# Rows of four tokens per partition, statistics by bn_aggr and a shorter warm-up in a gated mixer with routed experts

## What is computed

```python
xn = layernorm(x)                                   # per token over 128 channels
# mixer: six projections of x + (prev - x) * mix, a scan over time, a group norm of 8 channels
state = state * decay + alpha * k * v ; mixed = r * state
s = (groupnorm(mixed) * gn_w + gn_b) * g @ W_out.T + b_out
# experts: four rounds; 4 experts of 128 -> 512 -> 128, the best two of each token mixed by softmax
for r in range(4):
    logits = cur @ Wg[r] + bg[r]
    cur = cur + sum_e cw[:, e] * (gelu(cur @ W1[e] + b1[e]) @ W2[e] + b2[e])
out = x + s * silu(cur)
```

## Time and profile before

| what | value |
|---|---|
| median of 3 runs | 806.81 us (806.5 to 807.61) |
| the profiled execution's own time | 807.0 us |
| its span, first to last instruction | 804.9 us |
| PE busy | 793.4 us, 99% of the span |
| DVE busy | 711.7 us, 88% |
| ACT busy | 651.9 us, 81% |
| DMA, HBM traffic | 40.34 MB read, 2.36 MB written |

### The profile page before, as it was taken

How to read it: one execution, slowest core, us unless ns; L and a number is a source line. 1 busy time by engine, 2 the same in 40 slices (tenths; PEclk the granted TensorE clock), 3 DMA queues, 4 the chain that set the end, 5 groups by cost and what they waited for, 6 DMA issues and landing times.

```text
span 804.9 us, 10652 instructions
## 1 busy us (share of the span) xinstructions
PE 793.4 (99%) x3668; PEld 638.2 (79%) x3668; DVE 711.7 (88%) x1328; ACT 651.9 (81%) x912; POOL 114.8 (14%) x135
## 2 busy tenths in 40 slices
PE   7999999999999999999999999999999999999997
PEld 6778788887888878888788887888788887778785
DVE  6989888889998989889998889998989898998888
ACT  6899888877888877888788887888778877878775
POOL 0021111111111111111111111121111111111110
PEclk9999999999999999999999999999999999999999
DMA  9444362432532416333164422644236443174532
GB/s 258 121 89 133 67 188 49 106 92 40 146 83 61 101 31 155 96 57 89 33 152 98 101 40 42 142 105 100 46 62 155 100 118 66 28 184 118 132 66 52
DMA packets 44468, 78.50 MB, mean 98 GB/s; under 512 B 6656, under 2 KB 23552, under 8 KB 40448
## 3 DMA queue, kind: packets, MB, share of 16 engines
q0 software_dynamic: 18144, 33.04, 24.3%
q1 hardware_dynamic: 25136, 44.64, 17.1%
q10 hardware_dynamic: 1136, 0.16, 0.1%
HBM read 40.34 MB, written 2.36 MB: 53 GB/s over the span
## 4 chain that ended last, share of the span: by engine, by line
PE 88%; DVE 5%; ACT 2%; DMA 2%; issue 1%; SPq 0%; DVEq 0%; ACTq 0%
PE h_bank L910 13%; PE h_bank L906 13%; PE h_bank L907 13%; PE y_bank L971 13%; PE y_bank L967 13%; PE y_bank L966 13%; DVE g_lo L639 2%; PE p_bank L906 2%; PE p_bank L910 2%; PE p_bank L907 2%; PE r_bank L1005 1%; ACT g L401 1%; DMA cw_b<-in_w 1%; PE p_bank L936 1%; ACT g_hi L405 1%
## 5 line engine op out<-in xcount | busy, mean ns | idle before, releaser
L401 ACT ACTIVATE g<-h_bank,b_c 128x512 f32<-128x512 f32 x512 | 329.6, 682 | 71.8 <-PE h_bank L910 70.3
L639 DVE TENSOR_TENSOR g_lo<-g,g_hi 128x1024 fp32r<-128x1024 f32 x256 | 308.6, 1221 | 63.4 <-ACT g_hi L405 62.5
L405 ACT ACTIVATE g_hi<-g 128x1024 fp32r<-128x1024 f32 x256 | 271.9, 1062 | 8.1
L341 POOL DMA_DIRECT2D cur<-tmp x126 | 113.6, 902 | 677.7 <-DVE tmp L653 553.0
L906 PE MATMUL h_bank<-cur_hi,w_hi 128*128 128x512 f32 x512 | 205.9, 402 | 1.2 <-ACT g L401 0.7
L910 PE MATMUL h_bank<-cur_lo,w_hi 128*128 128x512 f32 x512 | 203.6, 398 | 0.0
L907 PE MATMUL h_bank<-cur_hi,w_lo 128*128 128x512 f32 x512 | 202.3, 395 | 0.0
L967 PE MATMUL y_bank<-g_hi,w_lo 128*128 128x512 f32 x508 | 200.6, 395 | 0.0
L966 PE MATMUL y_bank<-g_hi,w_hi 128*128 128x512 f32 x508 | 200.5, 395 | 0.0
L971 PE MATMUL y_bank<-g_lo,w_hi 128*128 128x512 f32 x508 | 139.3, 396 | 0.0
L910 PEld LDWEIGHTS h_bank<-cur_lo,w_hi 128*128 128x128 f32 x512 | 96.2, 188 | 23.5 <-DVE cur_lo L588 0.4
(11 more groups left out here) (133 smaller groups left out, 497.4 us busy)
## 6 DMA issues: line engine op xcount, KB each, us to landing
cur<-tmp POOLq DMA_DIRECT2D x126, 256.0 KB, 3.4
cw_b<-cw_scratch SPq DMA_DIRECT2D x31, 1024.0 KB, 5.1
cur<-in_x SPq DMA_DIRECT2D x8, 256.0 KB, 5.6
xn_t<-cur SPq DMA_DIRECT2D x8, 256.0 KB, 2.9
xr<-in_x SPq DMA_DIRECT2D x8, 256.0 KB, 3.2
out<-o SPq DMA_DIRECT2D x7, 256.0 KB, 2.4
cw_b<-in_w SPq DMA_DIRECT2D x4, 256.0 KB, 6.1
cw_b<-cw_scratch SPq DMA_DIRECT2D x1, 768.0 KB, 5.3
```

The costliest lines, as they stand in the source:

```text
L341: pool.dma_start(cur[:, block_of(s // E)], tmp[:, s % SUMS, :], accum_op=ALU.add).then_inc(summed, DMA)
L401: nc.scalar.activation(g[:, gb, ft * BLK:(ft + 1) * BLK], hb[ft][:, :], ACT.Gelu_apprx_tanh, bias=b1_c[:, e * FT + ft:e * FT + ft + 1]).th ...
L405: nc.scalar.activation(g_hi[:, gb, h], g[:, gb, h], ACT.Copy).then_inc(g_hi_done, 1)
L639: nc.vector.tensor_tensor(g_lo[:, gb, h], g[:, gb, h], as_f32(g_hi[:, gb, h]), ALU.subtract).then_inc(g_lo_done, 1)
```

## The change

The rows of x and of the output that a DMA moves become four tokens of one partition: partition p holds tokens 4p to 4p + 3 of its block, one row of 2048 bytes in memory (block 7: two tokens, 1024 bytes, for each half). A tile t then holds every fourth token, so `turn_normed` writes column t, t + 4, ... of its bank, and `turn_product` reads such columns of `th`; the rest of the kernel sees tokens in their old order. For blocks 0 and 1 mean and variance come from bn_aggr, block by block. The warm-up is 26 transposes and then 15, one behind each of DVE's first 15 linked steps.

```diff
-WARM_UP, FILL = 52, 4
+WARM_UP, FILL = 26, 4
+ROOT_CHAIN = 15
...
+        mv = sb("mv", [128, 2 * TPB, 2])
...
+        def by_partition(b, rows):
+            if b < NB - 1:
+                return rows.rearrange("(p t) d -> p t d", t=TPB)
+            return rows.rearrange("(n p t) d -> p n t d", n=2, t=TPB // 2)
+        def tokens_of(b, t):
+            if b < NB - 1:
+                return slice(t, BLK, TPB)
+            n, i = t // (TPB // 2), t % (TPB // 2)
+            return slice(n * HALF + i, (n + 1) * HALF, TPB // 2)
...
-                             x[c * BLK:(c + 1) * BLK, :].rearrange("(t p) d -> p t d", p=128)).then_inc(x_loaded[c], DMA)
+                             by_partition(c, x[c * BLK:(c + 1) * BLK, :])).then_inc(x_loaded[c], DMA)
...
-            sp.dma_start(out[(NB - 1) * BLK:(NB - 1) * BLK + BLK // 2, :].rearrange("(t p) d -> p t d", p=128),
+            sp.dma_start(out[(NB - 1) * BLK:(NB - 1) * BLK + BLK // 2, :].rearrange("(p t) d -> p t d", t=TPB // 2),
...
+            def norm_first():
+                for b in (0, 1):
+                    norm_stats((b,))
+                    for c in range(b * TPB, (b + 1) * TPB):
+                        last = nc.vector.bn_aggr(mv[:, c, :], stats[:, c, :])
+                    link(last)
+                h = tiles_of((0, 1))
+                link(nc.vector.tensor_scalar(veps[:, h], mv[:, :, 1], LN_EPS, None, ALU.add))
+                nc.vector.tensor_scalar(mean[:, h], mv[:, :, 0], 1.0, None, ALU.mult)
...
-            norm_stats((0, 1))
-            norm_spread((0, 1))
+            norm_first()
...
-                    ins = nc.tensor.transpose(pb[:, t * D:(t + 1) * D], xn_st[:, b % 2, t * D:(t + 1) * D], ident[:, :])
+                    ins = nc.tensor.transpose(pb[:, tokens_of(b, t)], xn_st[:, b % 2, t * D:(t + 1) * D], ident[:, :])
...
-                    ins = nc.tensor.transpose(rb[:, t * D:(t + 1) * D], th[:, b % 2, t * D:(t + 1) * D], ident[:, :])
+                    ins = nc.tensor.transpose(rb[:, t * D:(t + 1) * D], th[:, b % 2, tokens_of(b, t)], ident[:, :])
...
             for _ in range(WARM_UP):
                 nc.tensor.transpose(rb[:, 0:D], ident[:, :], ident[:, :])
+            for n in range(ROOT_CHAIN):
+                pe.wait_ge(dve_step, n + 1)
+                nc.tensor.transpose(rb[:, 0:D], ident[:, :], ident[:, :])
             turn_normed(0)
```

More of the change, by code:

```diff
@@ L226, in block_of, with by_tile @@
             return slice(k % NB * BLK, (k % NB + 1) * BLK)
+        def by_partition(b, rows):
+            if b < NB - 1:
+                return rows.rearrange("(p t) d -> p t d", t=TPB)
+            return rows.rearrange("(n p t) d -> p n t d", n=2, t=TPB // 2)
+        def by_tile(b, ap):
+            if b < NB - 1:
+                return ap.rearrange("p (t d) -> p t d", t=TPB)
+            return ap.rearrange("p (n t d) -> p n t d", n=2, t=TPB // 2)
+        def tokens_of(b, t):
+            if b < NB - 1:
+                return slice(t, BLK, TPB)
+            n, i = t // (TPB // 2), t % (TPB // 2)
+            return slice(n * HALF + i, (n + 1) * HALF, TPB // 2)
         block = ctx.enter_context(nc.Block())
@@ L232, in load_x @@
             def load_x(c):
-                sp.dma_start(cur[:, block_of(c)].rearrange("p (t d) -> p t d", t=TPB),
-                             x[c * BLK:(c + 1) * BLK, :].rearrange("(t p) d -> p t d", p=128)).then_inc(x_loaded[c], DMA)
+                sp.dma_start(by_tile(c, cur[:, block_of(c)]),
+                             by_partition(c, x[c * BLK:(c + 1) * BLK, :])).then_inc(x_loaded[c], DMA)
             def load_w1(e):
@@ L286, in load_x_again @@
                     sp.wait_ge(r_empty, r_jobs["end", b - 2] + 1)
-                sp.dma_start(xr[:, b % 2, :].rearrange("p (t d) -> p t d", t=TPB),
-                             x[b * BLK:(b + 1) * BLK, :].rearrange("(t p) d -> p t d", p=128)).then_inc(x_again[b % 2], DMA)
+                sp.dma_start(by_tile(b, xr[:, b % 2, :]),
+                             by_partition(b, x[b * BLK:(b + 1) * BLK, :])).then_inc(x_again[b % 2], DMA)
             def store(b):
                 sp.wait_ge(r_empty, r_jobs["end", b] + 1)
-                sp.dma_start(out[b * BLK:(b + 1) * BLK, :].rearrange("(t p) d -> p t d", p=128),
-                             o[:, b % 2, :].rearrange("p (t d) -> p t d", t=TPB)).then_inc(stored[b % 2], DMA)
+                sp.dma_start(by_partition(b, out[b * BLK:(b + 1) * BLK, :]),
+                             by_tile(b, o[:, b % 2, :])).then_inc(stored[b % 2], DMA)
             copy_block(0)
@@ L492, in _ @@
             act.wait_ge(half_done, 2)
-            act.dma_start(out[(NB - 1) * BLK + BLK // 2:NB * BLK, :].rearrange("(t p) d -> p t d", p=128),
+            act.dma_start(out[(NB - 1) * BLK + BLK // 2:NB * BLK, :].rearrange("(p t) d -> p t d", t=TPB // 2),
                           o[:, 1, BLK // 2:BLK].rearrange("p (t d) -> p t d", t=TPB // 2)).then_inc(last_stored, DMA)
@@ L1073, in _ @@
                 for t in range(2):
-                    col = n * HALF + t * D
-                    ins = nc.tensor.transpose(hb[n][:, t * D:(t + 1) * D], th[:, (NB - 1) % 2, col:col + D], ident[:, :])
+                    ins = nc.tensor.transpose(hb[n][:, t * D:(t + 1) * D], th[:, (NB - 1) % 2, tokens_of(NB - 1, 2 * n + t)],
+                                              ident[:, :])
                 ins.then_inc(half_turned, 1)
```

## The result

The changed kernel takes 810.72 us (median of 8 runs, 808.58 to 811.84) against 807.12 us of the kernel before (8 runs, 806.46 to 807.61): 1.0036 times as long, 95% interval 1.0026 to 1.0047, about 2.9 us more. (The ratio on record is not the quotient of the two medians, which lie 3.6 us apart. The profiled execution is one of the upper clump, 811.84 us with a span of 810.0, and so 5.1 us of span longer than the one before.

The account below looks back on a forecast made before the run. PE was taken to bound the kernel, busy in nearly all of it. Loads -0.4, statistics 0, warm-up 0, weights +0.1 and end 0 gave -0.3 us: 806.5 us from a median of 806.81, range 805.0 to 809.8.

Parts of the forecast that it names:

- What bounds the kernel: Whole kernel: PE busy 793.4 of 804.9 us, a full string in the middle; other engines can give only before and behind.
- The end: Last half block's store: 128 KB in 0.40 us for 0.45, perhaps 0.05 given back by a weight load; together 0.
- the first rival: Strided PSUM writes or weight reads slow PE's transposes: 809.6 us if one side doubles, 812.7 if both; chance 0.19.
- The loads of x: Start: larger rows land w1 of expert 2 sooner, sure 0.2 us plus a sixth of the hole; -0.4 us.
- the hole: DMA rate of 115 GB/s from 3.5 to 5.25 us; read as something of the start, not row size, so it stays.
- Statistics: Head, on DVE: bn_aggr stretch of 0.8 us replaces 1.04 us of seven operations; off the path, so 0.
- Warm-up: Head: fewer transposes leave PE half busy for some 2.5 us, never on the path; 0 us.
- Turning: Transposes with 16-byte steps: PSUM writes free, one weight load in each of seven turns waits 0.015 us; +0.1 us.
- The sign of being wrong: In the profile after: the forecast is wrong if a turn of four takes 0.6 us or more, for 0.44 before.
- A strided access costs PE: Rival on the transposes of seven turns and L928: doubled spacing, 809.6 us for one side, 812.7 for both; chance 0.19.
- The hole closes: Rival at the start: row size caused the slow DMA stretch, loads land 1.4 us sooner, 805.5 us; chance 0.18.
- The clock: Rival in the head: half-busy, then idle PE brings 1.2 GHz back by the first `up`, 808.6 us; chance 0.05.

Follow-up runs that it names:

- e5: Kernel before with only the second load of x and the stores in 2048-byte rows, product read side by side: 808.65 against 807.03 us, ratio 1.0026.
- e1: Kernel before with only the loads of x at the start in 2048-byte rows and strided PSUM writes: 807.45 against 807.03 us, ratio 1.0004.
- e3: Kernel before with only bn_aggr and the shorter warm-up, rows and transposes as before: 806.72 against 806.90 us, ratio 1.0000.
- e4: Kernel before with only the strided weight reads of the gated product, loads and stores in 512-byte rows: 807.53 against 807.03 us, ratio 1.0010.
- e2: Kernel before with the whole end part: second load of x and stores in 2048-byte rows, strided weight reads: 809.81 against 807.03 us, ratio 1.0035.
- e7: Changed kernel without its end part (keeps rows at the start, bn_aggr, shorter warm-up): 807.34 against 806.90 us of the kernel before, ratio 1.0004.
- e6: Changed kernel, gate load of turn 29 waiting until the accumulation of step 111 has landed: 807.60 against 806.90 us of the kernel before, ratio 1.0008.
- e10: Kernel before, gate load of turn 29 waiting until the accumulation of step 111 has landed, as a control: 806.81 against 806.79 us, ratio 0.9999.
- e9: Kernel before, 512-byte rows, gates of turn 29 spread ahead of block 2's store and block 4's second load: 813.30 against 806.79 us, ratio 1.0077.
- e8: e7 with ACT scaling blocks 0 and 1 ahead of the high part of w1 of expert 2: 806.77 against 806.90 us of the kernel before, ratio 0.9998.

## Why the prediction was wrong

It said 806.5 us with 805.0 to 809.8, and most likely no change; it is slower, and above the range. The step that failed is the sum's silence on what the changed DMAs at the end do to other DMAs. By its steps:

- **What bounds the kernel.** "Whatever comes off another engine there is worth nothing, and whatever is added to PE there counts in full" was right as far as it goes. What it left out is the step that failed: the change reshapes the stores and the second loads of x too, seven and eight DMAs of 256 KB on SP's queue in the last quarter, and the sum puts them at nothing without a reason: "The end" reckons only the last half block, and they were counted only as a possible gain ("less queueing"). They cost 2.1 us by themselves (e5), through a DMA of another queue: the accumulation of step 111 takes 5.3 to 6.2 us for 3.6, and PE's waits for the product grow from 1.7 to 3.9 (e5) and 4.7 us. The row was at hand: L928's waits for `th` said which chain has no slack there. That 810.72 lies near the 809.6 of the first rival is luck: the cost came by another way.
- **The loads of x.** Forecast -0.4; nothing (e1), and in the profile +0.24. The reading of the hole was right: it stayed. But then the sure 0.2 was no gain either, since what had moved in the hole before moved ahead of it now. The rate of such rows was put too low (326 GB/s for 378), which would have raised that term.
- **Statistics.** Forecast 0.8 us for the new stretch, measured 0.70 and four bn_aggr in 0.38; worth 0, as said (e3).
- **Warm-up.** 0, as said (e3).
- **The end.** Forecast 0; the last stores land some 0.2 us sooner (e5).
- **Turning.** Writes with a step: 0, as said. Weight reads with a step: that a longer load hides behind the transpose ahead of it, and one in each turn doesn't, was forecast; the size was not: 0.1 against 0.8 us (0.2 to 1.5) in e4. The sum gave the open load 0.015 us, but it shows its 70 ns whole: turns of four grow by 0.08 or 0.09 where they waited for data and by 0.03 elsewhere, 0.4 in all in the chain; the last turn adds some 0.07. The rest of the 0.8 is within the interval. The sign of being wrong, a turn of 0.6 us or more, was ill chosen: turns that wait for data took 0.66 us before (668.93), and take 0.75 now.
- **The rivals.** "A strided access costs PE" took the sign right and the place wrong: 0.03 us for each transpose would have been needed, and 0.02 and less was there. "The hole closes": no. "The clock" came, but in another place and as a consequence: PE idle for 3.6 us at 720, then 3.4 us at 1.2 GHz. In the head it came in six of the twelve profiles (last section), not in that of the changed kernel, and e3, whose profile has it, is no slower than the kernel before.

Shown by runs: that the end part holds the whole loss within the intervals (e1, e2, e3, e7), that the rows and not the reads hold most of it (e4, e5), and that the meeting of accumulation and gate load is the way (e6, with e10 as its control; e9 in the main). That the rows narrow the gap is seen in every profile at 607 us, and at 711 us wherever SP's order there is the old one. Only argued: how they do it. The profiles show both sides of it (SP's issues closer together, the accumulation ahead landing 7.8 us after its issue instead of 7.5), and no run parts them. The two clumps of runs fit a gap that decides within some tenths of a microsecond, and they fit as well a stretch at the lower clock, some 1.5 us, that follows the wait in some runs only; one run of each kernel is seen in a profile, of the upper clump each time, so this stays open. Untested too is whether the load of turn 28, 0.49 us behind an accumulation in every version, costs anything.

## What to carry to other kernels

A DMA that is "hidden anyway" can still cost: ask what else is on the DMA engines when it moves, and which transfer there has a reader without slack. A large load that no one needs for 20 us should wait for the small one that is needed now; one semaphore wait was worth 2.3 us (1.0036 to 1.0008). And where PE has no idle time except one wait of 0.7 us, look at everything that ends just before that wait.

## What the runs showed of the hardware

- A 256 KB accumulation from SBUF to SBUF takes 3.3 to 4.1 us from issue to landing when a 1 MB load follows it by 1.2 us or more, 4.8 to 6.2 when one follows by 0.7, 6.8 to 8.0 when one follows by 0.49, and 8.1 when one is 0.35 us ahead (e9, with two more DMAs behind). One that goes out 1.3 us behind such a load takes 5.1 (659.59 in the kernel before).
- Rows of 2048 bytes move at 378 GB/s while x streams in (12.5 to 16 us, in the changed kernel; 378 to 380 in e1, e7, e8), rows of 512 bytes at 290 (e3 and the kernel before).
- An fp32 transpose writes PSUM with a step of 16 bytes at no cost that can be told (273 ns each, before and after; e1 1.0004), against what the Trainium skill ("PSUM — Partial Sum Buffer", Specifications (TRN2)) says of non-contiguous access; as weights, a step of 16 bytes makes the load 70 ns longer, so there the rule of the Trainium skill ("SBUF — State Buffer", Specifications (TRN2)), two hits on each 16-byte line, points the right way.
- Four bn_aggr of one bn_stats row each take 0.38 us; the linked stretch with them is 0.70, against 1.04 for the seven operations.
- In the head too the granted clock fell in some profiles, with the long warm-up (e1, e2, e9) and the short one (e3, e6, e7) alike, and not in the other six. Stretches of e7:

```profile
11.30:14.70 3.40, 3.38 (x12) 2.68 (x13) 2.42 (x4) 3.34 (x8) 0.00 (x0) 0.50 1.08 364
14.80:18.00 3.20, 3.20 (x17) 2.62 (x17) 1.47 (x5) 3.09 (x5) 0.00 (x0) 1.00 1.08 349
```

  It lasted as long as the one at 724 us, fell on the first `up`, and moved the second one by some 0.3 to 0.5 us (19.09 here against 18.59 and 18.83). In all six it began at 11.3 to 13.3 us, behind PE's idle time of 1.4 to 1.7 us ahead of the first turn of four; but the changed kernel had 1.8 us there without it. Why in one execution and not in another is open.
